# One down part for a tile that two experts share: its hidden values weighted on GpSimd before they are split

## The chip, the core and the metric

The kernel runs on one core of a Trainium2 chip. The core has a matrix engine (TensorE, PE in the rows), VectorE (DVE), ScalarE (ACT), GpSimd (POOL) and a queue that issues DMAs (SyncE, SP). Matmul results land in PSUM, eight banks of 128x512 float32; everything else lies in SBUF. The metric is the device time of one execution in microseconds (us). Before the change it is 739.27 us, the median of three runs (738.42 to 740.68).

## What is computed

Four sequences of 512 tokens with 128 features go through feed-forward, attention, feed-forward ("macaron"). Each feed-forward is a mixture of one shared expert and eight routed ones, of which each token uses four:

```python
def _L0_ffn_ref(x, Wg, routing_bias, W1, W2, W3, Ws1, Ws2, Ws3):
    gate = jnp.einsum('bsd,ed->bse', x, Wg) + routing_bias
    _, top_idx = jax.lax.top_k(gate, K)                      # K = 4 of E = 8
    mask = jax.nn.one_hot(top_idx, E, dtype=gate.dtype).sum(-2)
    masked_gate = jnp.where(mask > 0, gate, -jnp.inf)
    weights = jax.nn.softmax(masked_gate, axis=-1) * mask
    out = _swiglu(x, Ws1, Ws2, Ws3)                          # hidden size 341
    h1 = jnp.einsum('bsd,ehd->ebsh', x, W1)
    h2 = jnp.einsum('bsd,ehd->ebsh', x, W2)
    eo = jnp.einsum('ebsh,edh->ebsd', jax.nn.sigmoid(h1) * h1 * h2, W3)
    return out + jnp.einsum('ebsd,bse->bsd', eo, weights)

x = x + 0.5 * ffn(layernorm(x))
x = x + attention(layernorm(x))     # causal, 16 heads of 64, softmax
x = x + 0.5 * ffn(layernorm(x))
```

Every product is made of three float16 matmuls (high by high, high by low, low by high), so each operand is split into a high and a low half after it is made.

## The kernel before

**Feed-forward.** It runs in eight chunks, c = 0 to 7: the first feed-forward of the four sequences, then the second. All experts are computed for all tokens. The nine experts' hidden units (341 each) lie packed, three experts to eight tiles of 128 units, so a chunk has 24 hidden tiles. Of each group's eight tiles, two hold units of two experts (tiles 2, 5, 10, 13, 18 and 21; `OWNERS` has two entries there). A tile goes through these steps:

- `hidden`: PE makes two banks, each of three matmuls with 512 columns (one bank for W1, one for W2). ACT takes the tanh of the first (L1095), DVE makes the gated product in two ops (L1280, L1284).
- `split_hidden`, two tiles later: ACT copies the product to float16 (`gluh`, L1102) and GpSimd makes the low half (`glul`, L826).
- `down`, four tiles later: twelve matmuls of 128 columns (four token blocks by three passes, L857 to L859, `bank<-w3h,gluh` and so on) add the tile to its expert's bank. A tile with two owners has two such parts, one with each expert's rows of W3, in two banks: 30 parts a chunk (`PARTS`).
- `collect`: when an expert's bank is complete, DVE adds it to the residual in four ops of 128x128, each weighted by the token's route to this expert (L1298).

**Router.** For each chunk PE makes the gate values and DVE ranks the eight experts by comparing all pairs: is greater (L1246), is equal (L1247), times "stands earlier" (L1254), sum (L1257), count (L1259), then the softmax of the four best (L1262 to L1274).

**Attention.** Per sequence 40 units (five units of scores for each of eight pairs of heads). For a unit: `scores` on PE (L980), `soften` on DVE (L1355), `bias` on GpSimd (L838), `exponentials` on ACT (L1119), `split_probs` on ACT (L1127) and GpSimd (L830, `paired`), `turn`, a DMA transpose issued by SP (L742, `pT<-paired`), `weigh`, PE's product with V (`bank<-vh,pT`), and `divide` on DVE (L1367, L1371). `heads` turns the finished heads (L821, L750) and `out` projects them.

**Order.** A planner (`Schedule`) writes one list of steps, and each engine issues its part of that list in this order. Feed-forward and attention are two streams: chunk 0 runs first; then every attention unit is followed by 0.55 of a feed-forward step (`FF_SHARES`) until attention is over; the rest of the feed-forward runs alone. `hold` keeps a PSUM bank for a sum over several steps, `bank` takes the free banks in turn. The order within one attention step is at the end of `attention`: `turn`, `weigh`, `scores`, `heads`, `soften`, then the feed-forward's share, then `out`, `exponentials`, `project`.

**Buffers and queues.** Six `glu` tiles, seven pairs of `gluh` and `glul`, four `probs`, `paired` and `pT`. Every DMA is issued by SP, in the order of the list.

## Time and profile before

| | |
|---|---|
| median of 3 runs | 739.27 us |
| the profiled execution | 738.95 us |
| its span in the trace | 737.2 us |
| PE, DVE, ACT, POOL busy | 91%, 87%, 79%, 66% |
| chunk 0 and the start of chunk 1, alone | 0 to 150 us |
| feed-forward beside attention | 150 to 620 us |
| feed-forward alone (chunks 6 and 7) | 620 to 737 us |

The last three rows are where the first and the last attention units stand in the trace. A busy share counts an engine as busy while any of its instructions is open. Matmuls overlap each other, so a busy PE need not be at its peak: the distance from one matmul's start to the next one's tells its real cost.

### The profile page before, as it was taken

The numbers are of one execution on the slowest core, as the hardware profiler recorded it, in microseconds if no ns is written. First come the engines' busy times: TensorE is split into PE (matmuls) and PEld (weight loads), VectorE is DVE, ScalarE is ACT, GpSimd is POOL, SyncE is SP. The second block draws the span as 40 slices with busy tenths as digits, with TensorE's granted clock in tenths as the row PEclk, the third lists the DMA queues.
The fourth block names the chain that finished last, engine by engine and source line by source line (L and its number), as shares of the span: only waits on it lengthen the run. The fifth ranks groups of instructions, "written<-read, shape, count | busy, mean of one in ns | idle before, by whom it ended". The sixth has DMA issues, their size and how long they took to land.

```text
span 737.2 us, 20502 instructions
## 1 busy us (share of the span) xinstructions
PE 673.0 (91%) x7601; PEld 447.1 (61%) x7601; DVE 640.2 (87%) x1728; ACT 580.9 (79%) x1155; POOL 483.0 (66%) x563
## 2 busy tenths in 40 slices
PE   2687979998899899899999799999999998999997
PEld 1365655565566666566666456665656765666665
DVE  1678998999999899899889999989999977889886
ACT  5787955697899888799888799889799993565553
POOL 3124655476788857688866679886588984555554
PEclk9988999998999999999999999999999999999999
DMA  7700000056589725578835579872479873000000
GB/s 207 221 1 1 2 1 1 2 80 104 92 134 141 129 44 98 98 128 137 132 74 83 91 116 131 136 124 44 88 131 144 145 121 54 16 2 1 15 3 15
DMA packets 216967, 60.58 MB, mean 82 GB/s; under 512 B 203682, under 2 KB 216100, under 8 KB 216868
## 3 DMA queue, kind: packets, MB, share of 16 engines
q1 hardware_dynamic: 216868, 59.28, 46.9%
q8 instruction: 60, 0.98, 0.5%
q14 instruction: 39, 0.32, 0.1%
HBM read 7.87 MB, written 1.05 MB: 12 GB/s over the span
## 4 chain that ended last, share of the span: by engine, by line
PE 37%; DVE 27%; ACT 18%; issue 9%; DMA 4%; POOL 4%; SPq 1%; DVEq 0%; ACTq 0%; POOLq 0%
PE bank L857 11%; PE bank L859 11%; PE bank L858 11%; ACT probs L1119 5%; DVE glu L1280 5%; DVE glu L1284 4%; DVE probs L1355 4%; DMA pT<-paired 3%; DVE xs L1298 3%; ACT glu L1095 3%; PE bank L980 3%; ACT gluh L1102 2%; POOL paired L830 1%; ACT xn L1061 1%; POOL glul L826 1%
## 5 line engine op out<-in xcount | busy, mean ns | idle before, releaser
L826 POOL TENSOR_TENSOR glul<-glu,gluh 128x512 f16<-128x512 f32 x192 | 222.4, 1160 | 125.5 <-ACT gluh L1102 124.9
L830 POOL TENSOR_TENSOR paired<-probs,paired 128x512 f16<-128x512 f32 x160 | 186.2, 1164 | 32.6 <-ACT paired L1127 31.3
L1095 ACT ACTIVATE glu<-bank,tanh_scale 128x512 f32<-128x512 f32 x192 | 130.8, 681 | 87.1 <-PE bank L859 86.0
L857 PE MATMUL bank<-w3h,gluh 128*128 128x128 f16 x960 | 174.2, 222 | 3.7 <-DVE xs L1298 2.4
L859 PE MATMUL bank<-w3h,glul 128*128 128x128 f16 x960 | 174.1, 222 | 0.0
L858 PE MATMUL bank<-w3l,gluh 128*128 128x128 f16 x960 | 174.1, 222 | 0.0
L1280 DVE SCALAR_TENSOR_TENSOR glu<-glu,bank 128x512 f32<-128x512 f32 x192 | 131.0, 682 | 36.6 <-ACT glu L1095 35.6
L1284 DVE SCALAR_TENSOR_TENSOR glu<-glu,bank 128x512 f32<-128x512 f32 x192 | 132.1, 688 | 20.5
L1119 ACT ACTIVATE probs<-probs,exp_bias 128x128 f32<-128x128 f32 (+3 forms) x256 | 131.7, 551 | 8.2 <-POOL exp_bias L838 8.1
L1355 DVE CUSTOM_DVE_ANT_0 probs<-bank,causal,score_scale 128x128 f32<-128x128 f32 (+3 forms) x256 | 127.9, 546 | 3.6 <-POOL paired L830 2.7
L1102 ACT ACTIVATE gluh<-glu 128x512 f16<-128x512 f32 x192 | 119.1, 621 | 12.1 <-DVE glu L1284 12.1
L857 PEld LDWEIGHTS bank<-w3h,gluh 128*128 128x128 f16 x960 | 95.4, 99 | 27.8 <-DVE xs L1298 2.9
L858 PEld LDWEIGHTS bank<-w3l,gluh 128*128 128x128 f16 x960 | 95.3, 99 | 19.1 <-issue 0.8
L1127 ACT ACTIVATE paired<-probs 128x512 f16<-128x512 f32 x160 | 100.7, 630 | 3.9
L859 PEld LDWEIGHTS bank<-w3h,glul 128*128 128x128 f16 x960 | 95.3, 99 | 0.0
L857 PE MATMUL bank<-vh,pT 128*128 128x65 f16 x640 | 74.5, 195 | 10.3 <-DMA pT<-paired 10.2
L857 PE MATMUL bank<-xnTh,w2h 128*128 128x512 f16 x192 | 74.2, 387 | 6.0 <-DVE ql L1155 6.0
L857 PE MATMUL bank<-xnTh,w1h 128*128 128x512 f16 x192 | 75.0, 390 | 4.5 <-DVE attn L1371 1.8
L858 PE MATMUL bank<-xnTl,w1h 128*128 128x512 f16 x192 | 74.5, 388 | 0.0
L857 PEld LDWEIGHTS bank<-vh,pT 128*128 128x128 f16 x640 | 59.7, 98 | 24.2 <-DMA pT<-paired 12.8
L859 PE MATMUL bank<-xnTh,w1l 128*128 128x512 f16 x192 | 74.3, 387 | 0.0
L858 PE MATMUL bank<-vl,pT 128*128 128x65 f16 x640 | 74.1, 195 | 0.0
(189 smaller groups left out, 1488.2 us busy)
## 6 DMA issues: line engine op xcount, KB each, us to landing
pT<-paired SPq DMA_TRANSPOSE x160, 3.2
attention_raw<-in_L_attn_W_qkv SPq DMA_DIRECT2D x6, 256.0 KB, 5.7
xs<-in_L_attn_inputs SPq DMA_DIRECT2D x4, 256.0 KB, 5.1
out<-xs SPq DMA_DIRECT2D x4, 256.0 KB, 2.9
vh<-in_L_ffn_W SPq DMA_DIRECT2D x6, 128.0 KB
pT<-in_L_ffn_W SPq DMA_DIRECT2D x6, 128.0 KB
raw_more<-in_L_ffn_W SPq DMA_DIRECT2D x4, 128.0 KB
attention_raw<-in_L_attn_W_out SPq DMA_DIRECT2D x2, 256.0 KB, 6.9
```

Of the source, the lines that this page charges most:

```text
L826: pool.tensor_tensor(glul[pair][:, :], g[:, :], gluh[pair][:, :], ALU.subtract).then_inc(glu_low)
L830: pool.tensor_tensor(paired[n % PAIRED][:, 1, :], probs[n % PROBS][:, :], paired[n % PAIRED][:, 0, :], ALU.subtract).then_inc(probs_low)
L857: pe.matmul(ps, high, mhigh, start=first, stop=False)
L858: pe.matmul(ps, high, mlow, start=False, stop=False)
L859: return pe.matmul(ps, low, mhigh, start=False, stop=last)
L1095: act.activation(g[:, :], psum[b1.bank][:, :], ACT.Tanh, scale=tanh_scale[:, j:j + 1]).then_inc(tanh_made)
L1102: act.activation(gluh[pair][:, :], glu[s["g"]][:, :], ACT.Copy).then_inc(glu_high)
L1119: e = act.activation(pr[:, at:at + (qt + 1) * P], pr[:, at:at + (qt + 1) * P], ACT.Exp, bias=exp_bias[:, gp % 2, qt, head:head + 1], scale ...
L1127: act.activation(paired[n % PAIRED][:, 0, :], probs[n % PROBS][:, :], ACT.Copy).then_inc(probs_high)
L1280: v.scalar_tensor_tensor(g[:, :], g[:, :], 1.0, psum[b1.bank][:, :], ALU.add, ALU.mult).then_inc(drained[b1.bank])
L1284: v.scalar_tensor_tensor(g[:, :], g[:, :], GLU_SCALE, psum[b2.bank][:, :], ALU.mult, ALU.mult).then_inc(drained[b2.bank])
L1355: made = v.tensor_tensor_reduce(out=pr[:, at:at + width], in0=psum[use.bank][:, ps_at:ps_at + width], in1=causal[:, NT - 1 - qt:NT, :].rea ...
```

## The change

A tile with two owners gets one down part instead of two, in chunks 1 to 7. For that its hidden values are weighted by the routes before they are split:

- The routes of a chunk (128 tokens by 36 columns) are turned by PE (`turn_route`), copied by ACT to `routeT`, stored by SP to memory (`store_route`) and read back once for each shared tile by two DMAs that repeat an expert's row of 512 routes over the partitions of its units (`widen`, five buffers in the third raw weight place, `raw_more` in the rows).
- GpSimd multiplies the tile's product in place by the widened routes (`weigh_hidden`, one step before its split). The ACT copy of that tile waits for it (`weighed`).
- The six weighted tiles and the shared expert's tiles 0 and 1 go to one bank (key `SHARED_SUM`) and are collected in one DVE op of 128x512. DVE's second product op takes a scale from SBUF in these tiles instead of a constant, and `share_scales` makes the scales once.
- Once, in chunk 1, GpSimd adds the two parts of W3 of each shared tile (`merge`).
- In chunks 1 to 7 the tiles go in another order (`LATER_TILES`), with the shared ones at places 8, 11, 14, 17, 20 and 22 and tile 1 last. The down part of a shared tile comes one step later than that of another.
- The ranking has three ops for five: subtract, is greater (against a smallest number for an earlier expert), count.
- In an attention step `weigh` and `heads` move behind the feed-forward's share, `out` before `weigh`.
- In chunk 0 the router starts two steps earlier (`ROUTE_STEP`).

```diff
+MIXED = [j for j in range(HT) if len(OWNERS[j]) > 1]
+LATER_TILES = [3, 4, 6, 7, 8, 9, 11, 12, 2, 14, 15, 5, 16, 17, 10, 19, 20, 13, 22, 23, 18, 0, 21, 1]
+SHARED_SUM = 0
+FIRST_DOWN = [(j, [(n, PARTS.index((j, n))) for n in OWNERS[j]]) for j in range(HT)]
+LATER_DOWN = [(j, [(SHARED_SUM if j in MIXED else OWNERS[j][0], PARTS.index((j, OWNERS[j][0])))])
+              for j in LATER_TILES]
...
-ROUTE_STEP = 6
+ROUTE_STEP = 4
 SPLIT_LAG = 2
 COLLECT_LAG = 1
+WIDES = 5
+WIDE_AHEAD = 5
+WEIGH_LAG = 1
+TURN_ROUTE_AT = 2
+STORE_ROUTE_AT = 4
+MERGE_AT = 7
...
+    def widen(self, c, j, wides):
+
+        self.add("widen", c=c, j=j, n=self.widened, last_raw=self.raw_left[RAWS - 1])
+        wides[j] = self.widened
+        self.widened += 1
+
+    def weigh_hidden(self, j, tiles, wides):
+        t = tiles[j]
+        self.add("weigh_hidden", g=t["g"], b2=t["b2"], n=wides[j])
+        self.weighed += 1
+        t["weighed"] = self.weighed
...
+    def turn_route(self, c):
+        use = self.bank()
+        self.add("turn_route", c=c, use=use)
+        self.route_turned[c % 2] = use
...
+        tiles, wides, collects, later = {}, {}, [], []
         routing = self.router(c)
+        plan = FIRST_DOWN if c == 0 else LATER_DOWN
+        keys = [key for _, of in plan for key, _ in of]
+        mixed = [] if c == 0 else [i for i, (j, _) in enumerate(plan) if j in MIXED]
+        to_widen, counts = list(mixed), defaultdict(int)
...
-                self.hidden(c, i, halves, tiles)
-                last_b2 = tiles[i]["b2"]
+                self.hidden(c, plan[i][0], halves, tiles)
+                last_b2 = tiles[plan[i][0]]["b2"]
+            if c > 0 and i == TURN_ROUTE_AT:
+                self.turn_route(c)
+            if c == 1 and i == MERGE_AT:
+                self.add("merge")
+            if c > 0 and i == STORE_ROUTE_AT:
+                self.add("store_route", c=c, use=self.route_turned[c % 2])
+            while i > STORE_ROUTE_AT and to_widen and to_widen[0] <= i + WIDE_AHEAD:
+                self.widen(c, plan[to_widen.pop(0)][0], wides)
...
+            if i - WEIGH_LAG in mixed:
+                self.weigh_hidden(plan[i - WEIGH_LAG][0], tiles, wides)
             if SPLIT_LAG <= i < HT + SPLIT_LAG:
-                self.split_hidden(i - SPLIT_LAG, tiles)
+                self.split_hidden(plan[i - SPLIT_LAG][0], tiles)
             done = []
-            parts = later
-            later = []
+            parts, later = later, []
             if DOWN_LAG <= i < HT + DOWN_LAG:
-                j = i - DOWN_LAG
-                parts = parts + [(j, OWNERS[j][0])]
-                later = [(j, n) for n in OWNERS[j][1:]]
-            for j, n in parts:
-                self.down(c, j, n, tiles, done)
+                j, of = plan[i - DOWN_LAG]
+                of = [(j, key, part, part == of[-1][1]) for key, part in of]
+                if i - DOWN_LAG in mixed:
+                    later = of
+                else:
+                    parts, later = parts + of[:1], of[1:]
+            for j, key, part, ends in parts:
+                counts[key] += 1
+                self.down(j, key, part, counts[key] == 1, counts[key] == keys.count(key), ends, tiles, done)
...
             turn(n)
-            weigh(n)
             scores(n)
-            heads(n)
+            soften(n)
             if n >= last - NU and n % 2 == 0:
                 next(ahead, None)
-            soften(n)
+            out(n)
             if n == last + PV_LAG - 1:
                 yield None
             yield shares[1] if n < last else shares[2]
-            out(n)
+            weigh(n)
             exponentials(n)
             project(n)
+            heads(n)
...
+                elif kind == "store_route":
+                    c, use = s["c"], s["use"]
+                    q.wait_ge(drained[use.bank], use.n + 1)
+                    sp.dma_start(weight_scratch[c], routeT[c % 2][:, :]).then_inc(route_stored, 16)
+                elif kind == "widen":
+                    j, n, left = s["j"], s["n"], s["last_raw"]
+                    rows = weight_scratch[s["c"]].rearrange("(n t) p -> n (t p)", t=NT)
+                    row = left_of(OWNERS[j][1])
+                    q.wait_ge(route_stored, 16 * s["c"])
+                    q.wait_ge(filled[left.bank], left.f + 1)
+                    if n >= WIDES:
+                        q.wait_ge(weighed, n - WIDES + 1)
+                    for expert, first, end in zip(OWNERS[j], (0, row), (row, P)):
+                        sp.dma_start(wide[n % WIDES][first:end, :],
+                                     rows[expert:expert + 1].broadcast_to([end - first, L])
+                                     ).then_inc(wide_in[n % WIDES], 16)
...
+                elif kind == "merge":
+                    q.wait_ge(down_done, len(PARTS))
+                    for w in (w3h, w3l):
+                        of = w[:, :, :].rearrange("p (g k) d -> p g k d", k=len(PARTS) // 3)
+                        before, this = (of[:, :, k:k + 5:4, :] for k in (2, 3))
+                        pool.tensor_tensor(before, before, this, ALU.add).then_inc(merged)
+                elif kind == "weigh_hidden":
+                    g, n, use = glu[s["g"]], s["n"], s["b2"]
+                    q.wait_ge(drained[use.bank], use.n + 1)
+                    q.wait_ge(wide_in[n % WIDES], 2 * 16 * (n // WIDES + 1))
+                    pool.tensor_tensor(g[:, :], g[:, :], wide[n % WIDES], ALU.mult).then_inc(weighed)
...
+                elif kind == "turn_route":
+                    c, use = s["c"], s["use"]
+                    q.wait_ge(route_made, c + 1)
+                    q.wait_ge(shared_scaled, 1)
+                    bank_free(use)
+                    pe.transpose(psum[use.bank][0:NE * NT, 0:P], route[c % 2][:, :, :].rearrange("p n t -> p (n t)"),
+                                 ident[:, :]).then_inc(filled[use.bank])
...
+                    if s["k"] >= HT and s["mixed"]:
+                        q.wait_ge(merged, 2)
...
+                    act.activation(routeT[c % 2][:, :], psum[use.bank][0:NE * NT, 0:P], ACT.Copy
+                                   ).then_inc(drained[use.bank])
...
+                    if s["weighed"]:
+                        q.wait_ge(weighed, s["weighed"])
+                    else:
+                        q.wait_ge(drained[b2.bank], b2.n + 1)
...
+                elif kind == "share_scales":
+                    q.wait_ge(tanh_scaled, len(GROUPS))
+                    chained(v.tensor_reduce(shared_unscale[:, :], unscale[:, :], AX.X, ALU.max))
+                    chain()
+                    chained(v.reciprocal(shared_scale[:, :], shared_unscale[:, :]))
+                    for i in range(2):
+                        chained(v.tensor_scalar(route[i][:, 0, :], ones[:, 0:NT], unscale[:, 0:1], None, ALU.mult))
+                    chain()
+                    chained(v.tensor_scalar(mixed_glu_scale[:, :], shared_scale[:, :], GLU_SCALE, None, ALU.mult))
+                    chain()
+                    v.tensor_tensor(shared_glu_scale[:, :], mixed_glu_scale[:, :], unscale[:, 0:1], ALU.mult
+                                    ).then_inc(shared_scaled)
...
-                    v.tensor_tensor(beats, rows_j, rows_i, ALU.is_gt)
-                    chained(v.tensor_tensor(ties, rows_j, rows_i, ALU.is_equal))
+                    chained(v.tensor_tensor(ahead_by, rows_j, rows_i, ALU.subtract))
...
-                    chained(v.tensor_tensor(ties, ties, earlier[:, :, :].unsqueeze(1).broadcast_to([P, NT, E, E]),
-                                            ALU.mult))
-                    chain()
-                    chained(v.tensor_tensor(beats, beats, ties, ALU.add))
-                    chain()
-                    chained(v.tensor_reduce(rank[:, :, :], beats, AX.X, ALU.add))
+                    if turned:
+                        q.wait_ge(filled[turned.bank], turned.f + 1)
+                    chain()
+                    chained(v.tensor_tensor(ahead_by, ahead_by, earlier[:, :, :].unsqueeze(1).broadcast_to([P, NT, E, E]),
+                                            ALU.is_gt))
+                    chain()
+                    chained(v.tensor_reduce(rank[:, :, :], ahead_by, AX.X, ALU.add))
...
+                    scale = GLU_SCALE
+                    if s["c"] and (s["j"] in MIXED or OWNERS[s["j"]] == [0]):
+                        q.wait_ge(shared_scaled, 1)
+                        scale = (mixed_glu_scale if s["j"] in MIXED else shared_glu_scale)[:, 0:1]
+                    v.scalar_tensor_tensor(g[:, :], g[:, :], scale, psum[b2.bank][:, :], ALU.mult, ALU.mult
...
+                    if c and n == SHARED_SUM:
+                        v.scalar_tensor_tensor(stream_of(b), psum[use.bank][:, :], shared_unscale[:, 0:1], stream_of(b),
+                                               ALU.mult, ALU.add).then_inc(drained[use.bank])
+                        continue
```

On GpSimd, beside the last attention units: `paired` (L830, now L920) is the low half of a unit's probabilities, `exp_bias` the bias, `glul` (L826, now L916) the low half of a hidden tile. Before:

```order
L830 TENSOR_TENSOR paired<-probs,paired 128x512
L838 TENSOR_TENSOR exp_bias<-neg_max,ln_scale 128x2x2
L830 TENSOR_TENSOR paired<-probs,paired 128x512
L826 TENSOR_TENSOR glul<-glu,gluh 128x512
L830 TENSOR_TENSOR paired<-probs,paired 128x512
L838 TENSOR_TENSOR exp_bias<-neg_max,ln_scale 128x2
L830 TENSOR_TENSOR paired<-probs,paired 128x512
```

The same engine and stretch now, where `glu<-glu,raw_more` (L912) is the new weighting of a shared tile:

```order
L920 TENSOR_TENSOR paired<-probs,paired 128x512
L928 TENSOR_TENSOR exp_bias<-neg_max,ln_scale 128x2x2
L920 TENSOR_TENSOR paired<-probs,paired 128x512
L912 TENSOR_TENSOR glu<-glu,raw_more 128x512
L916 TENSOR_TENSOR glul<-glu,gluh 128x512
L920 TENSOR_TENSOR paired<-probs,paired 128x512
L928 TENSOR_TENSOR exp_bias<-neg_max,ln_scale 128x2
L920 TENSOR_TENSOR paired<-probs,paired 128x512
L916 TENSOR_TENSOR glul<-glu,gluh 128x512
```

The weighting of the tile before stands ahead of the split of the tile two before, and the probabilities of the next unit stand behind both.

On VectorE, in one attention step: the product of a hidden tile (L1280, L1284), the division of finished heads (L1367, L1371), the scores of a unit (L1355). Before:

```order
L1280 SCALAR_TENSOR_TENSOR glu<-glu,bank 128x512
L1284 SCALAR_TENSOR_TENSOR glu<-glu,bank 128x512
L1367 RECIPROCAL inv_sum<-bank 128x4
L1371 TENSOR_TENSOR attn<-bank,inv_sum 128x2x128
L1355 ISA probs,neg_max<-bank,causal,score_scale 128x512
L1355 ISA neg_max 128x1
L1355 ISA probs,neg_max<-bank,causal,score_scale 128x512
L1355 ISA neg_max 128x1
L1155 SCALAR_TENSOR_TENSOR ql<-bank,qh 128x512
```

The same step now (L1400 and L1408 are the product, L1483 the scores, L1495 and L1499 the division):

```order
L1400 SCALAR_TENSOR_TENSOR glu<-glu,bank 128x512
L1408 SCALAR_TENSOR_TENSOR glu<-glu,bank 128x512
L1483 ISA probs,neg_max<-bank,causal,score_scale 128x512
L1483 ISA neg_max 128x1
L1483 ISA probs,neg_max<-bank,causal,score_scale 128x512
L1483 ISA neg_max 128x1
L1495 RECIPROCAL inv_sum<-bank 128x4
L1499 TENSOR_TENSOR attn<-bank,inv_sum 128x2x128
L1264 SCALAR_TENSOR_TENSOR ql<-bank,qh 128x512
```

The scores of a unit no longer stand behind the division of an earlier one, which itself follows PE's product with V.

On SP, at the start of chunk 5: `pT<-paired` and `attention_raw<-attn_pair` are the transposes of units and heads. Before:

```order
L742 DMA_TRANSPOSE pT<-paired 128x8x128 x5
L750 DMA_TRANSPOSE attention_raw<-attn_pair 128x8x128 x2
L742 DMA_TRANSPOSE pT<-paired 128x8x128 x10
L750 DMA_TRANSPOSE attention_raw<-attn_pair 128x8x128
L742 DMA_TRANSPOSE pT<-paired 128x8x128 x5
```

Now, with the store of the turned routes (L818) and the widened reads (L828):

```order
L812 DMA_TRANSPOSE attention_raw<-attn_pair 128x8x128
L804 DMA_TRANSPOSE pT<-paired 128x8x128 x3
L818 DMA weight_scratch<-routeT 36x128
L804 DMA_TRANSPOSE pT<-paired 128x8x128 x2
L828 DMA raw_more<-weight_scratch 85x512
L828 DMA raw_more<-weight_scratch 43x512
L812 DMA_TRANSPOSE attention_raw<-attn_pair 128x8x128
L804 DMA_TRANSPOSE pT<-paired 128x8x128 x2
L828 DMA raw_more<-weight_scratch 42x512
L828 DMA raw_more<-weight_scratch 86x512
```

A chunk beside attention puts one store and twelve reads between the transposes, and the first read waits until the store has landed.

## Rows read from the trace of the kernel before

**Rows 1.** The page: busy time by engine, and the chain that ended last.
```profile
PE 673.0 (91%) x7601; PEld 447.1 (61%) x7601; DVE 640.2 (87%) x1728; ACT 580.9 (79%) x1155; POOL 483.0 (66%) x563
PE 37%; DVE 27%; ACT 18%; issue 9%; DMA 4%; POOL 4%; SPq 1%; DVEq 0%; ACTq 0%; POOLq 0%
```

**Rows 2.** Busy us by stage: length, PE, PEld, DVE, ACT, POOL; clock, DMA.
```profile
60.00:124.00 64.00, 57.21 (x511) 38.74 (x510) 59.73 (x140) 44.73 (x88) 36.01 (x33) 0.92 0.00 1
150.00:620.00 470.00, 444.17 (x5495) 292.81 (x5496) 426.77 (x1227) 410.65 (x790) 357.95 (x404) 0.98 0.68 109
620.00:737.00 117.00, 112.08 (x1154) 77.22 (x1152) 96.96 (x216) 63.10 (x107) 60.37 (x54) 1.00 0.04 10
```

**Rows 3.** The same, of short stretches beside attention and of one alone.
```profile
200.00:210.00 10.00, 10.00 (x140) 6.64 (x139) 9.65 (x28) 9.21 (x18) 9.89 (x11) 1.00 0.73 127
540.00:580.00 40.00, 39.85 (x498) 25.16 (x497) 37.91 (x115) 39.52 (x77) 35.60 (x41) 1.00 0.88 142
630.00:650.00 20.00, 20.00 (x192) 13.12 (x191) 16.14 (x34) 12.05 (x20) 10.41 (x9) 1.00 0.06 15
```

**Rows 4.** Chain of waits, shares by line, of 150:620, then of 620:737.
```profile
by line: issue 11.0%; PE bank L857 9.7%; PE bank L858 8.7%; PE bank L859 8.7%; ACT probs L1119 7.6%; DVE probs L1355 5.6%; DMA pT<-paired 5.4%; PE bank L980 4.6%; DVE glu L1280 3.9%; DVE glu L1284 3.6%; ACT glu L1095 3.4%; ACT gluh L1102 2.
by line: PE bank L859 26.8%; PE bank L858 26.8%; PE bank L857 26.7%; issue 2.2%; POOL glul L826 1.9%; DVE glu L1280 1.7%; DVE xs L1298 1.7%; DVE glu L1284 1.2%; ACT glu L1095 1.1%; ACT xn L1061 1.1%; POOLq L542 1.0%; PE bank L922 0.9%; POOL
```

**Rows 5.** PE in order of time, chunk 6 (start, duration).
```profile
659.94 0.38 PE L857 MATMUL bank<-xnTh,w1h 128*128 128x512 f16 x1
...
661.24 0.22 PE L857 MATMUL bank<-w3h,gluh 128*128 128x128 f16 x1
...
661.85 0.22 PE L859 MATMUL bank<-w3h,glul 128*128 128x128 f16 x1
```

**Rows 6.** Tanh ops, one a hidden tile, by stage (count in brackets).
```profile
150.00:620.00 470.00, 69.98 (x104) 0.98 0.68 109
620.00:737.00 117.00, 33.48 (x49) 1.00 0.04 10
```

**Rows 7.** VectorE in order of time, chunk 6.
```profile
675.58 0.68 DVE L1280 SCALAR_TENSOR_TENSOR glu<-glu,bank 128x512 f32<-128x512 f32 x1
...
676.98 0.68 DVE L1280 SCALAR_TENSOR_TENSOR glu<-glu,bank 128x512 f32<-128x512 f32 x1
...
678.36 1.12 DVE L1298 SCALAR_TENSOR_TENSOR xs<-bank,route,xs 128x128 f32<-128x128 f32 x4
679.40 0.68 DVE L1280 SCALAR_TENSOR_TENSOR glu<-glu,bank 128x512 f32<-128x512 f32 x1
```

**Rows 8.** VectorE groups by shape (count | busy, mean ns | idle before).
```profile
L1247 DVE TENSOR_TENSOR xn<-gate 128x256 f32<-128x256 f32 x8 | 6.2, 777 | 0.0
L1257 DVE TENSOR_TENSOR xn<-xn 128x256 f32<-128x256 f32 x8 | 6.2, 769 | 0.3
L1307 DVE SCALAR_TENSOR_TENSOR xs<-bank,out_scale,xs 128x512 f32<-128x512 f32 x8 | 6.0, 750 | 0.6 <-PE bank L859 0.6
```

**Rows 9.** Line 1247 alone (ns: shortest, median, longest).
```profile
L1247 DVE TENSOR_TENSOR xn<-gate x8: 413/418/1384, 48.8 to 664.1; 128x256 f32<-128x256 f32 x8
```

**Rows 10.** GpSimd's two largest groups.
```profile
L826 POOL TENSOR_TENSOR glul<-glu,gluh 128x512 f16<-128x512 f32 x192 | 222.4, 1160 | 125.5 <-ACT gluh L1102 124.9
L830 POOL TENSOR_TENSOR paired<-probs,paired 128x512 f16<-128x512 f32 x160 | 186.2, 1164 | 32.6 <-ACT paired L1127 31.3
```

**Rows 11.** Waits (total us, times, longest).
```profile
PE bank L857 <- DMA pT<-paired: 10.2, 12, 2.5
PE bank L857 <- DVE ql L1155: 6.2, 3, 3.1
PE bank L980 <- DVE glu L1280: 4.3, 2, 4.0
```

**Rows 12.** DMA issues (KB each, us to landing).
```profile
pT<-paired SPq DMA_TRANSPOSE x160, 3.2
xs<-in_L_attn_inputs SPq DMA_DIRECT2D x4, 256.0 KB, 5.1
out<-xs SPq DMA_DIRECT2D x4, 256.0 KB, 2.9
```

**Rows 13.** The end of the program: GpSimd, then VectorE.
```profile
728.98 3.39 POOL L826 TENSOR_TENSOR glul<-glu,gluh 128x512 f16<-128x512 f32 x3 [0.80 <-ACT gluh L1102]
...
733.38 1.13 DVE L1298 SCALAR_TENSOR_TENSOR xs<-bank,route,xs 128x128 f32<-128x128 f32 x4 [1.09 <-PE bank L859]
```

55 lines of the change are left out of this document (36 added, 19 removed).

## Prediction

> **What bounds the kernel now.** I read the busy time of the page first, then the same by stage, then the chain of waits by stage, then the order of time where one engine looked full. The page shows four engines of 66 to 91% [rows 1]: no single one is the answer, so the stages have to be taken apart.
>
> From 620 us on, where the feed-forward runs alone, PE is busy 112 of 117 us, and L857 to L859 make 80% of the chain [rows 2, 4]. A hidden tile costs PE 1.30 us (659.94 to 661.24), a down part 0.67 us (661.24 to 661.85 are eleven of its twelve steps, so 0.056 each) [rows 5]. A chunk is 24 x 1.30 + 30 x 0.67 = 51 us of PE. VectorE needs 1.40 us a tile (675.58 to 676.98) and 1.04 us a collect (678.36 to 679.40) [rows 7]: 24 x 1.40 + 9 x 1.04 = 43 us, and the norm and router of the next chunk beside it in chunk 6. PE is the bound, VectorE the next.
>
> From 150 to 620 us, beside attention, PE is busy 94%, VectorE 91%, ACT 87%, GpSimd 76% [rows 2]. The chain is spread: L857 to L859 27.1%, scores on PE (L980) 4.6%, the ACT exponentials 7.6%, VectorE's lines 4 to 6% each, the transposes' landing 5.4% [rows 4]. In its dense stretches (540 to 580) ACT is busy 39.5 of 40 us; at 200 to 210 GpSimd is at 9.9 of 10 [rows 3]. From 60 to 124 us VectorE is busy 59.7 of 64 and is the bound [rows 2].
>
> **The change, part by part.** All sums are against the profiled execution, 738.95 us (span 737.2 and 1.75 around it); it is 0.3 below the median, so the forecast carries over.
>
> Down parts. Six parts a chunk go in seven chunks: 42 x 0.67 = 28 us of PE. Of the 12 in chunks 6 and 7, the last shared tile's down comes after the last hidden tile, where the chain goes through GpSimd's splits, so 11 x 0.67 = 7.4 us count. VectorE does not follow all the way: in the second half of chunk 6 it has 11 tiles (15.4), about four collects (4.1), norm and router (about 5), 24.5 us, where PE would need 11 x 1.97 + 1.5 = 23.2. I take off 1.3 and cost the last stage at -6; bounds -3 (VectorE binding everywhere) and -8.
>
> Beside attention there are 104 of the hidden tiles [rows 6], 104 / 4 = 26 of them shared, so 17.4 us of PE. L857 to L859 and L980 stand on the chain for 31.7% of 470 = 149 us of PE's 444, one third [rows 2, 4]. I take a third of 17.4: -6; bounds 0 (ACT alone decides) and -17.
>
> VectorE. A chunk's nine collects of four ops become eight and one op of 0.75 us instead of 1.04 [rows 7, 8]: -0.3. The ranking loses two ops of about 0.77 us mean [rows 8]: -1.5 a chunk in eight chunks. The first two routers lie in or at the edge of the stretch where VectorE binds: -3, against share_scales there, about eight small ops, which I price like the smallest rows shown (0.2 us): +1.5. The five beside attention remove 5 x 1.8 = 9 us of VectorE; it stands on the chain for 27% of its 87% of the page [rows 1], a third: -3. Bounds for both together -12 and +1.
>
> The ranking ops that go have a median of 418 ns and a longest of 1384 [rows 9], so something holds them now and then for almost a GpSimd op (1160 ns, [rows 10]). The Trainium skill has a rule that fits, in "SBUF — State Buffer", in the part on the engine ports and AXI ports: a VectorE op with two SBUF inputs and a GpSimd op exclude each other for their whole length. By that rule the 16 ops that go were worth 7 us if never blocked (16 x 0.42) and 22 if always; the rows' means give 12. The same rule speaks against the change, since GpSimd gets busier and the remaining ops are held oftener.
>
> GpSimd. It gets 42 weightings of 128x512 and, once, the merge of W3. No float32-out product of this size is in the trace; the nearest ops are the splits, 1.16 us each [rows 10], which I take, with bounds 0.6 and 2.3 us (half and twice that, since the bytes written double and nothing nearer is shown). 26 of them beside attention: 30 us, which lifts GpSimd from 358 to 388 of 470 us. GpSimd is on the chain for 4 of its 66% [rows 1], 6%, so 30 us would cost 2. In the stretches where it is at 9.9 of 10 it costs its full length: bounds +1 and +15, value +2.5. Alone, GpSimd has 10.4 of 20 us [rows 3] and two steps between the product and the ACT copy: nothing. In the Trainium skill, "GPSIMD Engine Reference", section 3.1, a float32 add of 2048 elements takes 4497 ns on GpSimd; a quarter of it, an estimate, is 1.12 us, and the sum would be the same by it.
>
> The wait that is added: ACT's copy of a shared tile waits for the weighting. Behind it on ACT stand the exponentials of the next unit. The weighting is issued a step before, and waits for VectorE's product only; I cost it at nothing, and +8 if it fails in every third of 26 tiles by one microsecond.
>
> DMAs. 84 reads and 7 stores pass SP's queue. Store and read take about 2.9 + 5.1 = 8 us by the rows of that size [rows 12]; the turned routes are ready in step 3 and the first weighting is in step 9, at least 12 us later. The first read holds SP until the store has landed, up to 2.9 us, and the transposes behind it. A transpose has four steps until `weigh` wants it. Zero; +5 if it always shows. The 10.7 MB more are 18% on 60 MB.
>
> Attention's order. PE waits 10.2 us for transposes in 12 places [rows 11], and 5.4% of 470 = 25 us of the chain are their landing [rows 4]. With `weigh` behind the feed-forward's share each has half a step (over a microsecond) more, and the scores no longer stand behind it. I take half: -5; bounds 0 and -25.
>
> Banks. The shared sum holds a bank from step 13 to 28 of each chunk, so two of eight are held where mostly one was. Today's bank waits are small (6.2 and 4.3 us [rows 11]); I take +2, bounds 0 and +10.
>
> The end. GpSimd's last three splits run back to back (728.98 to 732.4) and a collect of 1.13 ends the program [rows 13]. One weighting joins them, one op of 0.75 replaces the collect: 0, from -0.5 to +1.2.
>
> Sum: -6 - 6 - 1.5 - 3 + 2.5 - 5 + 2 + 0 = -17, and -1 for the two shared parts fewer in chunk 1 before 150 us: -18. 738.95 - 18 = 721.
>
> **Rivals.** (a) Attention's stage does not move, because ACT is full in it (39.5 of 40, [rows 3]) and nothing is taken from ACT. For it: the chain of that stretch is ACT and VectorE. Against: ACT is busy only 87% of the whole stage. Then only the last stage, the first chunks and a little remain: -6 - 1.5 - 1 - 1 = 729.5.
>
> (b) The reordering is the larger part: PE no longer waits for transposes, scores come earlier, and the stage tightens towards ACT. ACT's 411 us at 95% are 432, and two thirds of the way there from 470 are -25; with the rest of the sum 738.95 - 8.5 - 25 = 705.5.
>
> (c) Slower: GpSimd becomes what attention waits for. A weighting stands ahead of a split of a hidden tile and of the next unit's probabilities and itself waits for VectorE; then the transpose, PE's product and the exponentials behind the ACT copy are late. It decides from the point where a shared tile costs this stage 0.7 us more than now (18 / 26). If a full weighting shows and the 0.67 of PE are not felt, it is 26 x 1.16 = +30 against the -8.5 outside and -5 of the order: 738.95 + 16.5 = 755; at half of it 742. I name 742. For it: 9.9 of 10 us at 200. Against: 24% idle over the stage, and before its `paired` ops GpSimd itself waits 31 us for ACT [rows 10], so it is seldom the late one.
>
> (d) The widened rows come late (SP's queue or DMA share, already 0.88 in 540 to 580 [rows 3]), so the saving is given back: 735.
>
> **How the numbers follow.** Forecast 721, own range 713 to 728: 0.46. (a) 729.5: 0.22. (b) 705.5: 0.13. (c) 742: 0.12. (d) 735: 0.07. A measurement of this kernel tells 0.3%, 2.2 us, from no change. Slower by more than that is most of (c) and a little of (d): 0.12; within it the rest of both: 0.06; faster 0.82. The range leaves out the far halves of (b) and (c): 704 to 739.
>
> **What would show it.** 504 fewer matmuls of 128 columns on PE; chunks 6 and 7 alone some 6 us shorter, with VectorE near 90% there; the wait of PE for `pT` below 5 us; 42 GpSimd products near 1.16 us, none with a long wait for a DMA; ACT's copies not waiting for them; the router's ranking 1.5 us shorter a chunk. I am wrong if the stage beside attention is no shorter than now while the last one is (then ACT or GpSimd holds it), or if GpSimd's products take 2 us or more.

## The result and the profile after

The changed kernel takes 775.23 us, the median of four runs (771.03 to 775.94). Its ratio to the kernel before is 1.047 (95% interval 1.043 to 1.051): 36 us slower, where 18 us faster was forecast. The profiled execution took 775.55 us, its span 773.8.

The page of the changed kernel, busy time and the chain that ended last, beside [rows 1]:

```profile
PE 663.3 (86%) x7104; PEld 422.6 (55%) x7104; DVE 638.0 (82%) x1697; ACT 581.3 (75%) x1162; POOL 537.0 (69%) x607
PE 28%; DVE 27%; DMA 13%; ACT 12%; issue 10%; POOL 9%; SPq 0%; DVEq 0%; POOLq 0%; ACTq 0%
```

Only GpSimd has clearly more to do (+54 us), and every other engine is idle for longer. The new entry is DMA: 13% of the chain where it was 4%. By stage (length, PE, PEld, DVE, ACT, POOL, clock, DMA share, GB/s), beside [rows 2]:

```profile
60.00:124.00 64.00, 54.66 (x482) 35.50 (x482) 58.61 (x136) 45.31 (x89) 35.97 (x33) 0.95 0.04 13
150.00:655.00 505.00, 441.14 (x5226) 279.95 (x5226) 425.14 (x1209) 410.61 (x794) 391.14 (x433) 0.97 0.84 115
655.00:773.00 118.00, 107.78 (x995) 69.89 (x991) 97.56 (x204) 65.74 (x113) 78.00 (x68) 0.97 0.12 37
```

The stage beside attention is 505 us long instead of 470. It moves about the same GB/s as before, yet the DMA engines are busy 84% of it instead of 68%: in each microsecond more packets stand open, and they carry hardly more. The last stage is about as long as before (113.1 us against 114.1, counted from the first tanh of chunk 6). The waits of the whole run (total us, times, longest), beside [rows 11], and its DMAs, beside [rows 12]:

```profile
PE bank L947 <- DMA pT<-paired: 39.5, 28, 3.8
ACT paired L1236 <- DMA pT<-paired: 33.2, 17, 3.7
PE bank L947 <- DVE xs L1426: 8.0, 7, 3.8
ACT gluh L1211 <- POOL glu L912: 7.4, 8, 2.2
```

```profile
raw_more<-weight_scratch SPq DMA_DIRECT2D x21, 172.0 KB
raw_more<-weight_scratch SPq DMA_DIRECT2D x21, 170.0 KB
pT<-paired SPq DMA_TRANSPOSE x160, 3.8
raw_more<-weight_scratch SPq DMA_DIRECT2D x21, 86.0 KB
raw_more<-weight_scratch SPq DMA_DIRECT2D x21, 84.0 KB
...
out<-xs SPq DMA_DIRECT2D x4, 256.0 KB, 9.4
```

PE's wait for transposes went from 10 to 40 us, and ACT now waits too, for a `paired` buffer that a transpose still reads. SP in order of time shows where (start, time of the issue, what):

```profile
219.35 1.38 SPq L804 DMA_TRANSPOSE pT<-paired  x1
220.83 0.82 SPq L828 DMA_DIRECT2D raw_more<-weight_scratch  x2
221.74 7.03 SPq L804 DMA_TRANSPOSE pT<-paired  x2
228.83 0.85 SPq L828 DMA_DIRECT2D raw_more<-weight_scratch  x2
229.78 5.54 SPq L804 DMA_TRANSPOSE pT<-paired  x2
```

One transpose takes SP 1.38 us to issue; the two behind the reads take 7.03 together. PE, and in the next fence ACT, stand still at the end of that:

```profile
229.99 0.20 PE L947 MATMUL bank<-vh,pT 128*128 128x65 f16 x1 [1.64 <-DMA pT<-paired]
```

```profile
230.03 0.63 ACT L1236 ACTIVATE paired<-probs 128x512 f16<-128x512 f32 x1 [2.48 <-DMA pT<-paired]
```

The time from issue to landing over all 160 transposes, in the changed kernel:

```profile
L804 SPq DMA_TRANSPOSE pT<-paired x160: 1231/1272/5882, 154.2 to 648.3; - x160
...
DMA to landing us min/median/max: 3.0/3.8/9.8
```

and in the kernel before, where none took over 5.2 us:

```profile
DMA to landing us min/median/max: 3.0/3.2/5.2
```

Of the transposes, the 29 that SP issues within 4 us behind a read land after a median of 6.8 us, those with no read near after 3.3.

### The profile page after: what moved, and what is told of

It is laid out like the page before. It is cut to its first block, busy times and chain, and to the rows that moved or that the text cites. A ratio compares the mean times of both kernels' runs of the same rounds, so it can differ in the third digit from the quotient of the medians.

```text
span 773.8 us, 19728 instructions
## 1 busy us (share of the span) xinstructions
PE 663.3 (86%) x7104; PEld 422.6 (55%) x7104; DVE 638.0 (82%) x1697; ACT 581.3 (75%) x1162; POOL 537.0 (69%) x607
## 4 chain that ended last, share of the span: by engine, by line
PE 28%; DVE 27%; DMA 13%; ACT 12%; issue 10%; POOL 9%; SPq 0%; DVEq 0%; POOLq 0%; ACTq 0%
DMA pT<-paired 13%; PE bank L947 9%; PE bank L949 8%; PE bank L948 8%; DVE glu L1400 5%; DVE glu L1408 4%; DVE xs L1426 4%; POOL paired L920 3%; DVE probs L1483 3%; POOL glul L916 2%; PE bank L1079 2%; ACT probs L1228 2%; ACT glu L1194 2%; ACT paired L1236 2%; POOL glu L912 1%
## 5 line engine op out<-in xcount | busy, mean ns | idle before, releaser
L916 POOL TENSOR_TENSOR glul<-glu,gluh 128x512 f16<-128x512 f32 x192 | 222.1, 1160 | 92.2 <-ACT gluh L1211 91.9
L920 POOL TENSOR_TENSOR paired<-probs,paired 128x512 f16<-128x512 f32 x160 | 185.7, 1162 | 55.6 <-ACT paired L1236 54.2
L1400 DVE SCALAR_TENSOR_TENSOR glu<-glu,bank 128x512 f32<-128x512 f32 x192 | 130.6, 680 | 41.0 <-ACT glu L1194 40.1
L947 PE MATMUL bank<-w3h,gluh 128*128 128x128 f16 x792 | 144.5, 223 | 6.1 <-POOL glul L916 4.5
L948 PE MATMUL bank<-w3l,gluh 128*128 128x128 f16 x792 | 144.2, 222 | 0.0
L949 PE MATMUL bank<-w3h,glul 128*128 128x128 f16 x792 | 144.0, 222 | 0.0
L1483 DVE CUSTOM_DVE_ANT_0 probs<-bank,causal,score_scale 128x128 f32<-128x128 f32 (+3 forms) x256 | 127.6, 546 | 19.8 <-POOL paired L920 12.1
L947 PE MATMUL bank<-vh,pT 128*128 128x65 f16 x640 | 76.2, 196 | 40.4 <-DMA pT<-paired 39.5
L1408 DVE SCALAR_TENSOR_TENSOR glu<-glu,bank 128x512 f32<-128x512 f32 x136 | 93.6, 688 | 15.0 <-DVE glu L1400 0.5
L947 PEld LDWEIGHTS bank<-w3h,gluh 128*128 128x128 f16 x792 | 79.2, 100 | 28.3 <-POOL glul L916 7.3
L948 PEld LDWEIGHTS bank<-w3l,gluh 128*128 128x128 f16 x792 | 79.0, 100 | 15.7 <-issue 2.0
L949 PEld LDWEIGHTS bank<-w3h,glul 128*128 128x128 f16 x792 | 79.0, 100 | 0.0
L948 PE MATMUL bank<-vl,pT 128*128 128x65 f16 x640 | 75.8, 195 | 0.0
```

The source lines that it names most:

```text
L916: pool.tensor_tensor(glul[pair][:, :], g[:, :], gluh[pair][:, :], ALU.subtract).then_inc(glu_low)
L920: pool.tensor_tensor(paired[n % PAIRED][:, 1, :], probs[n % PROBS][:, :], paired[n % PAIRED][:, 0, :], ALU.subtract).then_inc(probs_low)
L947: pe.matmul(ps, high, mhigh, start=first, stop=False)
L948: pe.matmul(ps, high, mlow, start=False, stop=False)
L949: return pe.matmul(ps, low, mhigh, start=False, stop=last)
L1400: v.scalar_tensor_tensor(g[:, :], g[:, :], 1.0, psum[b1.bank][:, :], ALU.add, ALU.mult).then_inc(drained[b1.bank])
```

## The experiments

Medians are in us, of four executions (five with the shared parts in chunks 6 and 7 only, two with narrow reads). Ratios are to the kernel before in the same job (its medians were 739.5, 741.3, 739.9 and 740.4).

| run | median | ratio (95%) |
|---|---|---|
| changed, old attention order | 785.5 | 1.061 (1.056 to 1.065) |
| before, new attention order | 732.5 | 0.988 (0.984 to 0.992) |
| changed, reads made once | 732.5 | 0.989 (0.986 to 0.993) |
| changed, no weighting, no reads | 721.0 | 0.974 (0.969 to 0.979) |
| changed, reads cut by 16 rows | 733.3 | 0.990 (0.987 to 0.993) |
| changed, reads cut 64 and 64 | 732.8 | 0.989 (0.987 to 0.992) |
| changed, narrow reads | 731.9 | 0.988 (0.984 to 0.991) |
| before, new order and ranking | 723.9 | 0.977 (0.975 to 0.980) |
| shared parts in chunks 6, 7 only | 723.9 | 0.979 (0.977 to 0.982) |
| second parts left out | 713.5 | 0.965 (0.962 to 0.967) |
| changed by 16, product aside | 734.3 | 0.993 (0.991 to 0.996) |
| changed by 16, weighting after split | 732.3 | 0.990 (0.988 to 0.992) |
| second parts left out, new tile order and bank | 717.5 | 0.971 (0.969 to 0.973) |
| second parts left out, changed start | 713.6 | 0.965 (0.963 to 0.968) |

**1. Order, reads or GpSimd.** The theories were the reads (R), the new place of `weigh` in the ring of four `pT` buffers (O) and GpSimd's extra op (G). The old order put back in the changed kernel:

```diff
             turn(n)
+            weigh(n)
             scores(n)
-            soften(n)
+            heads(n)
...
-            out(n)
+            soften(n)
...
-            weigh(n)
+            out(n)
             exponentials(n)
             project(n)
-            heads(n)
```

> The changed kernel with the old order inside an attention step (weigh and heads before the feed-forward's share, out after it). Theory R (reads): transposes issued within 4 us behind a widened read land after 6.8 us where others take 3.3, so the order matters little: 770 to 776 us, PE's wait for pT still 30 us or more. Theory O (order): weigh now frees a pT buffer half a step later, SP issues the transposes later and the ring of four closes; with the old order back most of the 36 us return: 742 to 752. Theory G (GpSimd's extra op is what attention waits for): 770 to 776 as well.

It measured 785.5, slower still by 10 us and outside the range of all three theories: PE's wait for `pT` rose from 39.5 to 48.7 us, so the new order helps in the changed kernel too. The same edit the other way, alone in the kernel before:

> The kernel before with only the new order inside an attention step. Theory R: no reads, so no loss; 734 to 742 us, by the prediction's own step (-5) rather below 739. Theory O: slower, 752 to 770, with PE's wait for pT above 25 us.

732.5, with a wait of 3.1 us for `pT`: theory O is dead, and the order is worth 7 to 9 us. Next the reads:

```diff
-                    q.wait_ge(route_stored, 16 * s["c"])
-                    q.wait_ge(filled[left.bank], left.f + 1)
                     if n >= WIDES:
-                        q.wait_ge(weighed, n - WIDES + 1)
+                        continue
+                    q.wait_ge(route_stored, 16 * s["c"])
+                    q.wait_ge(filled[left.bank], left.f + 1)
```

> The changed kernel in which only the first five widened reads are made and all later tiles are weighted by those stale routes: everything but 37 of 42 pairs of reads stays. Theory R: the loss goes with them: 720 to 740 us, transposes land in 3.3 us. Theory O and theory G: 768 to 776, since order and GpSimd's ops are as in the changed kernel.

732.5: the 37 pairs of reads that are gone cost 43 us. In the profiled executions 40 of them lie beside attention, where 25 of these pairs are; the 12 in chunks 6 and 7 cost 3 together. So a pair costs 1.6 us where transposes stand behind it. (The same edit also lets GpSimd wait for the first reads only and each store for the one before.) And without GpSimd's op (the steps `widen` and `weigh_hidden` are not planned; the hidden tiles stay unweighted):

```diff
-        self.add("widen", c=c, j=j, n=self.widened, last_raw=self.raw_left[RAWS - 1])
...
-        self.add("weigh_hidden", g=t["g"], b2=t["b2"], n=wides[j])
```

> The changed kernel without the widened reads and without GpSimd's weighting of the shared tiles (their routes are left out of the result); one down part, order, banks and router as in the changed kernel. Against the run with reads made once it prices GpSimd's 42 ops of 1.28 us and the wait of ACT for them: theory G says 15 us or more less than that run, theory R 0 to 8 less. Theory O: still above 760.

721.0, 11.5 us less than with stale weights, between the 0 to 8 of theory R and the 15 of theory G. So the op costs more than I thought, and the reads cost nearly four times as much.

**2. What is wrong with the reads.** The new theory, K, looks at their rows: 85 and 43, or 42 and 86.

```diff
-                    for expert, first, end in zip(OWNERS[j], (0, row), (row, P)):
+                    a, b = row // 16 * 16, row + (P - row) // 16 * 16
+                    one, two = OWNERS[j]
+                    for expert, first, end in ((one, 0, a), (one, a, row), (two, row, b), (two, b, P)):
```

> The changed kernel with each widened read cut where a multiple of 16 rows ends: four reads a tile (80 and 5 or 32 and 10 rows, then 32 and 11 or 80 and 6) in place of two of 85 and 43 or 42 and 86. Theory B (the 256 KB and their reading from one row of memory are slow whatever the cut): 765 to 776. Theory N (the number of DMAs on SP's queue costs): slower than the changed kernel, 780 or more. The Trainium skill, "DMA: Bandwidth & Descriptors", in the section on why a DMA increments its semaphore by 16, states that the number of engines is the largest up to 16 that divides the rows; by it these reads are on 16, 5, 10, 11 and 6.

733.3, with twice as many DMAs and the same bytes. Theories B and N are out. SP at the same place in this run:

```profile
220.79 1.65 SPq L830 DMA_DIRECT2D raw_more<-weight_scratch  x4
222.54 2.62 SPq L804 DMA_TRANSPOSE pT<-paired  x2
225.21 1.70 SPq L830 DMA_DIRECT2D raw_more<-weight_scratch  x4
227.00 2.75 SPq L804 DMA_TRANSPOSE pT<-paired  x2
```

Four reads take SP 1.65 us instead of 0.82 for two, but the two transposes behind them 2.62 instead of 7.03. PE's wait for `pT` in it:

```profile
PE bank L949 <- DMA pT<-paired: 5.5, 5, 2.1
```

and the landing times of its transposes:

```profile
DMA to landing us min/median/max: 3.0/3.3/5.3
```

The two controls cut the reads at row 64, and, in the other kernel, shorten all reads but the first of each buffer to 128 of 512 columns:

```diff
-                    row = left_of(OWNERS[j][1])
+                    row = P // 2
```

```diff
-                        sp.dma_start(wide[n % WIDES][first:end, :],
-                                     rows[expert:expert + 1].broadcast_to([end - first, L])
+                        cols = L if n < WIDES else P
+                        sp.dma_start(wide[n % WIDES][first:end, 0:cols],
+                                     rows[expert:expert + 1, 0:cols].broadcast_to([end - first, cols])
```

> The changed kernel with the two reads of a shared tile cut at row 64 instead of at the experts' border (so 21 or 22 rows get the other expert's weight): the same 84 reads and the same bytes. Theory K: 730 to 740. Theories B and N: 770 to 778.

> The changed kernel with the rows of all reads but the first ten cut to 128 of 512 columns (the rest of the weights is stale): the same reads and row counts, a quarter of the bytes. 
732.8 with the same 84 reads and the same bytes, cut elsewhere; 731.9 with the bad row counts but a quarter of the bytes in each, better than the 738 to 750 that theory K had for it. So neither the number of reads nor their row counts alone cost anything here; a few engines with many long packets do. A measured 2 KB packet of a read is open for 0.084 us in the median, so 43 of them one behind the other are 3.6 us, near the 3.5 us by which the transposes behind a read are late. The trace does not name the engine of a packet, but it shows one at work. In the changed kernel, behind the reads issued at 220.83, the DMA engines do this (the DMA share and GB/s stand last):

```profile
225.00:228.00 3.00, 2.82 (x35) 1.68 (x33) 2.86 (x7) 2.55 (x5) 2.71 (x4) 1.00 0.07 26
```

A share of 0.07 is about one engine of 16. From 225.03 to 228.47 the trace has 43 packets of 2 KB, one behind the other, 0.080 us apart: the read of 43 rows. The two transposes issued at 221.74 and 225.66 land only behind that, at 229.95 and 235.46. Where the narrow reads stand in the same way, their packets of 512 bytes start 0.024 us apart, so 43 of them are 1 us. The Trainium skill states the rule, in "DMA: Bandwidth & Descriptors", in the section on why a DMA increments its semaphore by 16: a DMA from such a queue is split over the largest number of engines up to 16 that divides its row count, which is 1 for 43 rows, 2 for 86, 5 for 85, 14 for 42 and 16 for 64. The measurements agree: one engine in the row above for 43 rows, and no loss with 64.

**3. What the parts, the ranking and the weighting are worth.** The ranking in three ops, added to the new order in the kernel before:

```diff
-                    v.tensor_tensor(beats, rows_j, rows_i, ALU.is_gt)
-                    chained(v.tensor_tensor(ties, rows_j, rows_i, ALU.is_equal))
+                    chained(v.tensor_tensor(ahead_by, rows_j, rows_i, ALU.subtract))
...
-                                            ALU.mult))
-                    chain()
-                    chained(v.tensor_tensor(beats, beats, ties, ALU.add))
+                                            ALU.is_gt))
```

> The kernel before with the new order in an attention step and the ranking in three ops, nothing else: two down parts for a shared tile, no weighting, no reads. The order alone measured 732.5. By the prediction's step the ranking is worth 1.5 us in each of the two routers where VectorE binds and a third of that in five others, 4 to 6 us: 727 to 729. If the ranking lies beside other work everywhere: 731 to 733.

723.9, below both ranges: the ranking was worth more than I had it for. This version beats both kernels. The ranking's remaining ops in it, beside [rows 8]:

```profile
L1253 DVE TENSOR_TENSOR xn<-xn,earlier 128x256 f32<-128x256 f32 x8 | 4.9, 618 | 0.0
L1246 DVE TENSOR_TENSOR xn<-gate 128x256 f32<-128x256 f32 x8 | 3.6, 452 | 0.0
```

The two ops that are gone were 12.4 us of VectorE, and the whole got 8.2 us shorter by the ratios. Then the part scheme only where nothing runs beside it, with the scales and the merge of W3 made there too (the first line of the edit):

```diff
-        plan = FIRST_DOWN if c == 0 else LATER_DOWN
+        plan = FIRST_DOWN if c < SHARED_FROM else LATER_DOWN     # SHARED_FROM = 6
```

> One down part for a shared tile only in chunks 6 and 7, which run without attention, with the reads cut by 16; the new attention order and the ranking in three ops everywhere; the scales made at the start of chunk 6 and the router of chunk 0 where it was. The run with order and ranking alone measured 723.9 and took 114.1 us from the start of chunk 6 to the end; the run with reads by 16 took 111.7. If the part scheme pays where PE is the bound and GpSimd half idle: 720.5 to 722.5. If its gain there is eaten by the scales on VectorE: 723 to 725.

723.9, no better than without it: from the first tanh of chunk 6 to the end its profiled execution took 114.1 us (607.0 to 721.1), as the run without (610.4 to 724.5). So in this form the scheme gives nothing even there. That is the range of the second case, but whether the scales, the merge or the weighting ate the gain was not tested apart. What PE's time alone is worth:

```diff
-        plan = FIRST_DOWN if c == 0 else LATER_DOWN
+        plan = FIRST_DOWN if c == 0 else [(j, of[:1]) for j, of in FIRST_DOWN]
```

> Order and ranking as in the changed kernel, the old tile order and banks, and in chunks 1 to 7 the second down part of each shared tile left out (its contribution is missing from the result): 28 us less on PE, four collect ops per expert as before, no weighting, no reads. Against 723.9 for the same with the parts. Theory V (beside attention VectorE and ACT decide, PE's time passes through at a small share): 718 to 721, of which 3 to 5 us are in the last stage. Theory P (PE's time counts a third beside attention, as the prediction had it, and the changed kernel lost it to banks or tile order): 710 to 714.

713.5. Theory P holds: 28 us of PE are worth 9 to 10, of which 6.7 lie in the last stage (107.4 us from chunk 6 to the end against 114.1). Beside attention the profiled execution is 5.9 us shorter, a third of the 17.4 us of PE that go there. Is the weighting ACT's wait or GpSimd's time?

```diff
-                    pool.tensor_tensor(g[:, :], g[:, :], wide[n % WIDES], ALU.mult)
+                    pool.tensor_tensor(wide[n % WIDES], g[:, :], wide[n % WIDES], ALU.mult)
...
-                    if s["weighed"]:
-                        q.wait_ge(weighed, s["weighed"])
-                    else:
-                        q.wait_ge(drained[b2.bank], b2.n + 1)
+                    q.wait_ge(drained[b2.bank], b2.n + 1)
```

> The changed kernel with the reads cut by 16 (733.3), where GpSimd writes the weighted product into the widened tile instead of the hidden one and ACT's copy does not wait for it (so the shared tiles stay unweighted in the result): the same GpSimd ops, no added wait. If the 11.5 us of the weighting are GpSimd's time: 732 to 734. If they are ACT's wait for it: 722 to 725.

734.3: with no wait for it on ACT the time stays. Then the place in the queue, with `split_hidden` issued ahead of it:

```diff
-            if i - WEIGH_LAG in mixed:
-                self.weigh_hidden(plan[i - WEIGH_LAG][0], tiles, wides)
...
+            if i - WEIGH_LAG in mixed:
+                self.weigh_hidden(plan[i - WEIGH_LAG][0], tiles, wides)
```

> The changed kernel with the reads cut by 16 (733.3), GpSimd's weighting of a tile placed behind the split of the tile before instead of ahead of it. If the weighting's 11.5 us come from what queues directly behind it (the split, whose down part PE reaches two steps later): 725 to 729. If it is GpSimd's time as such beside attention, wherever it stands: 731 to 736.

732.3, so a place one op later gives nothing either. That does not yet show how GpSimd's time reaches the others: in the last run ACT's wait for the weighting rose from 8.0 to 33.6 us, and the next unit's bias and probabilities stand behind the weighting in every run. The traces show two ways that it can take. The first is those ops: with the weighting (reads made once) VectorE waits 13.2 us for `paired` and ACT 6.1 for the bias, without it 8.5 and 2.8. The second is VectorE itself, which is busy 7 us longer for the same 1697 instructions (3.5 us in the run with the weighting after the split), first with the weighting and then without:

```profile
PE 651.6 (89%) x7104; PEld 415.7 (57%) x7104; DVE 635.4 (87%) x1697; ACT 580.9 (79%) x1162; POOL 536.1 (73%) x607
```

```profile
PE 647.6 (90%) x7104; PEld 415.1 (58%) x7104; DVE 628.2 (87%) x1697; ACT 579.8 (81%) x1162; POOL 486.3 (68%) x565
```

The time is in the small ops of the router and the norm: 128x32 products that took 3.4 us in eight took 5.0. The prediction had said that the remaining ops would be held oftener, and gave it no price. How the 11 us divide between the two ways was not measured.

Last, what is between 713.5 and 721.0, in two kernels made from the one without the second parts:

```diff
-        plan = FIRST_DOWN if c == 0 else [(j, of[:1]) for j, of in FIRST_DOWN]
+        plan = FIRST_DOWN if c == 0 else LATER_DOWN
```

```diff
-ROUTE_STEP = 6
+ROUTE_STEP = 4
...
+                if g == len(GROUPS) - 1:
+                    self.add("share_scales")
```

> As the run with the second parts left out (713.5), but with the changed kernel's tile order and its one bank for the shared expert and the six shared tiles (collected in four ops). If the 7.5 us between that run and the one without weighting (721.0) are the bank held over 16 of 28 steps and the order: 719 to 722. If they are the scales, the earlier first router, the turning and storing of routes: 712 to 715.

> As the run with the second parts left out (713.5), but with the changed kernel's start: the router of chunk 0 two steps earlier and the eight small ops of the shared scales in chunk 0. If the start costs what the prediction priced (+1.5): 714.5 to 716. If it is the larger part of the 7.5 us: 718 to 721.

717.5 and 713.6: tile order and held bank make 4 to 5 us (less than the 719 expected if they were all of it), the start nothing. Order and bank were not tested apart. PE's wait for a bank that VectorE's collect frees, with the second parts left out and then with the new order and bank as well but no weighting:

```profile
PE bank L1077 <- DVE xs L1424: 3.6, 5, 1.1
```

```profile
PE bank L946 <- DVE xs L1425: 6.8, 8, 3.3
PE bank L1078 <- DVE xs L1425: 2.6, 4, 1.1
```

## Why the prediction was wrong

Ratios times 739.5 make a ledger across the jobs (each step is good to 2 to 3 us, so the two smallest are not clear of nothing):

| step | forecast | measured | from |
|---|---|---|---|
| attention's order | -5 | -8.6 | order alone |
| ranking | -5.5 | -8.2 | order and ranking, against order |
| second down parts | -13 | -9.4 | second parts left out, against order and ranking |
| banks and tile order | +2 | +4.7 | new tile order and bank, against the last |
| start, turning and storing routes, scaled products, merge, later down parts, one collect | +1 | +2.4 | no weighting, against the last |
| weighting on GpSimd | +2.5 | +11.2 | reads once, against no weighting |
| reads, as such | 0 | +0.6 | by 16, against reads once |
| reads, by their row counts | 0 | +42 | changed, against by 16 |
| sum | -18 | +35 | |

The same in the profiled executions, one of each, as the length from the first `pT` transpose to the first tanh of chunk 6 (beside attention) and from there to the end. One execution is good to some 2 us:

| run | beside attention | last stage |
|---|---|---|
| before | 472.5 | 114.1 |
| new attention order | 464.4 | 114.1 |
| order and ranking | 457.6 | 114.1 |
| second parts left out | 451.7 | 107.4 |
| and new tile order and bank | 457.8 | 107.6 |
| changed, no weighting, no reads | 458.3 | 109.2 |
| changed, reads made once | 466.9 | 110.2 |
| changed, reads cut by 16 | 468.5 | 111.7 |
| changed | 506.5 | 113.1 |

**The step that failed** is "DMAs": "A transpose has four steps until `weigh` wants it. Zero; +5 if it always shows." I took the landing of 256 KB loads of 128 rows [rows 12] for reads of 43 and 86 rows, which SP's own list showed as such, and asked only whether the weights would be in time. They are: GpSimd never waits long for them. What came late were the transposes behind them, and that cost 42 us, 38 of them beside attention. Rival (d) had the right queue but the wrong DMA: it let the widened rows be late and took the saving back, 735, a third of what the late transposes cost. It looked at the share of bytes and not at how the bytes spread over the engines. The measured 775 lies beyond every case that I named.

**The weighting** was mis-sized. 42 ops of 1.28 us on GpSimd (1.16 was taken; this row is of the changed kernel) cost 11 us and not 2.5:

```profile
L912 POOL TENSOR_TENSOR glu<-glu,raw_more 128x512 f32<-128x512 f32 x42 | 53.9, 1284 | 4.6 <-DVE glu L1408 4.5
```

I had multiplied added GpSimd time by GpSimd's 6% on the chain. That share says what GpSimd's present work holds up; added work held up more, here 21% of its length, and VectorE's longer ops had no term. The 11 lie inside the bounds of the term (+1 to +15), far from its value. Rival (c) had part of this mechanism, with a larger price (its own terms give 740.5 for the half case, where it names 742).

**The ranking** was under-priced in all (-8.2 for -5.5, the collects left out), and put in the wrong place. Of the forecast 3 us were in the first two routers, where VectorE was called the bound, and the start did not get shorter: the first transpose is issued at 153.3 us without the new ranking and at 152.8 with it. Beside attention 2.5 were forecast, a third of VectorE's time, and 6.8 came. In the version with order and ranking the chain is PE 38%, VectorE 34%, ACT 10%, so VectorE's time counts over a third of the whole, not only where it is the fullest engine.

**The down parts** were right in mechanism and size where they were tested alone: 5.9 us beside attention for the forecast 6, and 6.7 in the last stage for 6, in profiled executions (by the medians the whole is 9.4 for 13, so part of that is scatter). **The order** was right in mechanism, PE's wait for transposes falling from 10.2 to 3.1 us with it alone, and gave 8.6 for the forecast 5. In the last stage only 2.4 us are left with weighting and good reads (111.7 us against 114.1): new tile order and bank take 0.2 of the 6.7, the step to the kernel without weighting 1.6, the weighting 1.0, the reads 1.5. A scale read from SBUF costs VectorE 60 ns a product; the first row is of the 14 products of tiles 0 and 1, the second of those with a constant, in the changed kernel:

```profile
L1408 DVE SCALAR_TENSOR_TENSOR glu<-glu,shared_glu_scale,bank 128x512 f32<-128x512 f32 x14 | 10.5, 747 | 1.5
...
L1408 DVE SCALAR_TENSOR_TENSOR glu<-glu,bank 128x512 f32<-128x512 f32 x136 | 93.6, 688 | 15.0 <-DVE glu L1400 0.5
```

56 products at 0.06 us are 3.4 us more of the engine that is next in line, 1 us of it in the last stage, which the prediction had at nothing.

**Open.** Whether bank or tile order makes the 4.7 us; how the weighting's 11 us divide between the ops that queue behind it and VectorE's longer ops; why the scheme in chunks 6 and 7 alone gains nothing, where the same two chunks take 111.7 us in the changed kernel with reads cut by 16. There the scales and the merge are made long before.

## What to carry to other kernels

Write down the row count of every DMA that a change adds, and ask what shares its queue: here a small read on one or two engines delayed the transposes behind it, and the DMA that was late was not the new one. With four engines 76 to 94% busy beside attention [rows 2], this kernel gave back a third of the time taken from PE and two thirds of that taken from VectorE, and lost a fifth of what was added to GpSimd. So 28 us off PE (9 won) for 54 us on GpSimd (11 lost) does not pay here even with good reads, and the helper ops come on top. Measure the parts of a bundled change apart: here the two small ones (order and ranking, 17 us together) were worth more than the large one, and hid in a loss.

## What was not expected of the hardware

- The same 256 KB a tile, read from memory in two DMAs of 43 and 85 (or 42 and 86) rows, cost 42 us of 733 that they do not cost in two DMAs of 64 rows or in four cut at multiples of 16.
- Behind such reads the issuing queue is held too: the longest issue of a transpose was 5.9 us, against a median of 1.27; with the reads cut by 16 the longest was 2.6, and 2.5 in the kernel before.
- VectorE was busy 3.5 to 8 us longer for the same instructions where GpSimd had 42 ops more (631.7 to 636.4 us, the reads not being late, against 628.2).
- Where the transposes were late, the mean granted TensorE clock was lower too. The spans of the changed kernel and, second, of the one with the reads cut by 16:

```profile
core 0: 773.8 us, clock 0.959
```

```profile
core 0: 734.2 us, clock 0.974
```

A mean of 0.959 is 1.2 GHz instead of 2.4 for 2 x 0.041, some 8% of the span, against 5% in the second. PE's longer waits go with it; how much of the 42 us is the clock was not measured.
